# A state-space mixer and an expert network on one core: 68 identity transposes instead of 44 ahead of the last batch's row transposes

## What is computed

```
x = x + mixer(ctx_1024, layernorm(x))
x = x + ffn(layernorm(x))
```

```
scores = softmax(x @ gate_w.T);  topk_w, topk_i = top_k(scores, 6)
y = einsum('eci,eih->ech', silu(g) * u, w_down)
out = y summed over the 6 choices + silu(x @ sw_gate) * (x @ sw_up) @ sw_down
```

## Time and profile before

| | us |
|---|---|
| median of 3 executions | 1032.78 (1031.4 to 1037.14) |
| the profiled execution | 1031.32 |
| its span, first to last instruction | 1029.6 |
| TensorE matmul busy | 860.5 (84%) |
| VectorE busy | 603.9 (59%) |
| GpSimd busy | 565.4 (55%) |
| ScalarE busy | 498.0 (48%) |

### The profile page before, as it was taken

One profiled execution on the slowest core, in us unless ns is written; L12 is line 12 of the kernel. 1 busy time (PEld: TensorE's weight loads), 2 busy tenths in 40 slices (PEclk: granted clock), 3 DMA queues, 4 the chain that ended last, 5 costly groups with the idle time before them and its releaser, 6 DMA issues.

```text
span 1029.6 us, 12583 instructions
## 1 busy us (share of the span) xinstructions
PE 860.5 (84%) x4213; PEld 479.6 (47%) x4213; DVE 603.9 (59%) x862; ACT 498.0 (48%) x895; POOL 565.4 (55%) x318
## 2 busy tenths in 40 slices
PE   6375656667999786999789988999999988999984
PEld 3153445455455374545555474444444443444431
DVE  4589899889888988998798853222122211111111
ACT  4589545797776788766766223222122211221210
POOL 0387998987988988979777601122222212213111
PEclk9568655589899988999899979999999999999998
DMA  8633344334434553333637675999999999999995
GB/s 284 231 123 123 125 159 147 123 123 166 129 123 144 176 165 117 123 123 104 224 111 241 226 274 208 402 394 386 399 395 388 398 397 396 396 386 399 387 387 137
DMA packets 68411, 250.66 MB, mean 243 GB/s; under 512 B 10506, under 2 KB 13078, under 8 KB 68092
## 3 DMA queue, kind: packets, MB, share of 16 engines
q1 hardware_dynamic: 54740, 226.09, 58.4%
q0 software_dynamic: 7712, 18.88, 7.5%
q10 hardware_dynamic: 5896, 4.90, 1.5%
HBM read 230.67 MB, written 19.17 MB: 243 GB/s over the span
## 4 chain that ended last, share of the span: by engine, by line
PE 51%; DVE 16%; DMA 10%; issue 6%; ACT 6%; SPq 3%; POOL 2%; POOLq 0%; ACTq 0%; DVEq 0%
PE ps L683 13%; PE ps L886 10%; PE ps L678 9%; PE ps L694 8%; PE ps L910 6%; DVE ps L1272 6%; DMA arena<-in_L_ffn_w_down 5%; DVE arena L1279 4%; SPq L569 3%; DVE arena L1298 2%; ACT ps L1081 2%; PE ps L919 1%; DMA out_rows<-routes,idxs 1%; DVE arena L1272 1%; DMA out_rows<-xn,idxs 1%
## 5 line engine op out<-in xcount | busy, mean ns | idle before, releaser
L1516 POOL TENSOR_TENSOR arena<-arena 128x1024 f32<-128x1024 f32 x128 | 300.0, 2359 | 57.2 <-DMA arena<-bc_rows 40.0
L678 PE MATMUL ps<-ident,arena 128*128 128x128 f32 (+2 forms) x1408 | 238.5, 321 | 84.5 <-DVE ps L1280 39.8
L678 PEld LDWEIGHTS ps<-ident,arena 128*128 128x128 f32 (+2 forms) x1408 | 199.3, 177 | 190.1 <-issue 85.8
L1081 ACT ACTIVATE ps<-arena,An 128x511 f32<-128x511 f32 x256 | 165.2, 680 | 109.5 <-DVE ps L1280 93.4
L1272 DVE TENSOR_TENSOR_SCAN ps<-ps,arena 128x1024 f32<-128x1024 f32 x82 | 187.6, 2287 | 15.5 <-ACT ps L1081 14.7
L886 PE MATMUL ps<-arena 128*64 128x352 f32 x984 | 158.7, 461 | 7.7 <-issue 3.9
L683 PE MATMUL ps<-xnT,sw 128*128 128x512 f32 x320 | 152.1, 619 | 12.7 <-ACT arena L1042 11.8
L1530 POOL DMA_INDIRECT arena<-xn_rows,idu x32 | 34.1, 1066 | 208.6 <-DVE wcol L1426 149.1
L1521 POOL TENSOR_TENSOR arena<-arena 128x1024 f32<-128x1024 f32 x46 | 108.4, 2356 | 49.0 <-DVE arena L1272 49.0
L1433 DVE TENSOR_TENSOR arena<-arena,ps 128x352 f32<-128x352 f32 x32 | 16.7, 522 | 171.1 <-PE ps L886 171.1
L886 PEld LDWEIGHTS ps<-arena 128*64 128x64 f32 x984 | 73.2, 137 | 80.8 <-issue 71.3
(11 more groups left out here) (166 smaller groups left out, 903.6 us busy)
## 6 DMA issues: line engine op xcount, KB each, us to landing
arena<-bc_rows SPq DMA_DIRECT2D x128, 512.0 KB, 4.8
arena<-in_L_ffn_w_down SPq DMA_DIRECT2D x59, 768.0 KB, 23.0
arena<-in_L_ffn_w_gate SPq DMA_DIRECT2D x64, 704.0 KB, 23.5
arena<-in_L_ffn_w_up SPq DMA_DIRECT2D x59, 704.0 KB, 23.3
arena<-in_x SPq DMA_DIRECT2D x4, 1024.0 KB, 6.8
xn_rows<-xn ACTq DMA_DIRECT2D x4, 1024.0 KB, 6.4
out_rows<-arena SPq DMA_DIRECT2D x4, 1024.0 KB, 5.2
extra<-in_L_ffn_w_up SPq DMA_DIRECT2D x5, 704.0 KB, 22.3
```

Of the source, the lines that this page charges most:

```text
L678: return nc.tensor.matmul(dst, src, ident[0:k, 0:k], is_transpose=True, **kw)
L1081: a = nc.scalar.activation(ps[:, 2 * (c % 2) + n, 1:L], dt[k][:, 1:L], ACT.Exp, scale=An[:, k, NB * g + n:NB * g + n + 1])
L1516: G.tensor_tensor(R[c % RING], dtu[k][:, None, :].to_broadcast([P, NB, L]), Brep[n % REPS], ALU.mult)\
```

## The change

The constant that sets the number of transposes of the identity in the job `pe warm` goes from 44 to 68. Nothing else differs.

```
-TAILFILL = 44
+TAILFILL = 68
```

## The result

| | before | after |
|---|---|---|
| median, us (20 executions each) | 1032.42 (1027.42 to 1037.14) | 1027.56 (1025.07 to 1032.08) |
| ratio, 95% interval | | 0.9959 (0.9944 to 0.9975) |
| the profiled execution, us | 1031.32 | 1027.87 |
| its span, us | 1029.6 | 1026.1 |

The change makes the kernel faster, by 0.41%: 4.2 us by the ratio, 4.9 by the medians. I had forecast 1026.0 with a range of 1023.0 to 1033.5 and a gain of 6.0 us. The measured median is inside that range and just past the end of the forecast's own, narrower one (1023.5 to 1027.5).

A forecast was written before the change was run, and what follows sets the result against it. DMA bounds the expert stream, but its restart waits on TensorE's routing at half clock; profiled 1031.32 minus 6.0 gives 1025.3, with the median's offset 1026.8, forecast 1026.0 between; range 1023.0 to 1033.5, the forecast's own 1023.5 to 1027.5.

The forecast's parts named there:

- The mechanism: Before the last batch's row transposes: 24 added transposes fill TensorE's 2.45 us idle time, cost about 0, and prevent the clock's fall.
- the replay: Last batch's routing recalculated at full TensorE clock, from row transposes at 604.04 us to first tokens at 631.9, 6.0 us earlier.
- The score store: Last batch's store of scores, which the first gather awaits: starts right behind the row store, lands at 626.5 us.
- Rival (a): The score store still lands at 630.2 us and holds the first gather: tokens only 3.1 us earlier, time 1028.2; chance 0.18.
- So for about 13.6 us (...) a bound TensorE runs at 1.2 GHz instead of 2.4: Last batch's routing, 604.45 to 618.1 us: half clock while TensorE is the bound; removing it was to give 6.0 us.
- within 0.5%: Outcome class for the whole kernel's time: a change under some 5.2 us, not told from no change; chance 0.45.
- The idle time's length: TensorE's gaps before a clock fall: 2.22 us was followed by one, 1.93 us not; 2.45 us counted as falling side.
- Rival (c): The idle gap before the row transposes does not cause the low clock, so nothing is gained: 1031.3 us; chance 0.05.
- Rival (b): The clock falls anyway at 604 to 608 us, during row transposes and logits with short waits: 1031.3 us; chance 0.12.
- The expert stream passes an earlier start on: Expert weight stream: starting the first pair earlier ends the rest, same bytes at the same rate, earlier by the same amount.
- rival (d): Expert weight stream restarted at another moment meets other waits and loses half the gain: 1028.3 us; chance 0.05.
- slower rival (e): In the fill, TensorE is already at 1.2 GHz, so the 24 added transposes put 5.1 us on the path: 1036.4 us; chance 0.05.

## Why the prediction came out as it did

**The mechanism was right.** In the changed kernel's first profile the added transposes fill the idle time and cost nothing (7.59 us for 68, 7.6 forecast). The clock does not fall. From the row transposes to the mask's end it is 8.84 us (8.5 forecast), to the run of 20 9.19 (8.9), to the tokens 28.26 (27.9). The 0.3 us went in small waits for the copies before the logits' end; from there on the replay was right. Gain of the stage in this pair of profiles: 33.87 - 28.26 = 5.6 us, 6.0 forecast.

**The score store** was the sharpest test of the replay, and it came out 0.8 us late. I put its landing at 626.5 and it came at 626.6, but this profile starts the stage 0.63 us early, so that agreement is luck. Behind the first row transposes the landing was forecast at 22.5 us and came at 23.2, the gather at 23.4 and came at 24.3; its data took 3.9 us, not 3.5. The term that was too small is the time from the store's first packet to its landing, 7.2 us in the prediction: ScalarE's queue turns from the row store's large packets to the score store's small ones at about 618.5 (52 packets with 0.11 MB in 617 to 618, 47 with 0.04 MB in the next us, 71 with 0.02 MB in the one after), which leaves 8.1. The order that the Trainium skill's rule on rings gives (DMA: Bandwidth & Descriptors, Queues, rings and completion order), row store first, agrees with these packets; the rule gives no landing time. Standing behind the row store is not what makes this store slow: in the profile of before only 4 packets were left on the queue from 619.5 on, the store was issued at 619.73, and it still took 10.5 us. Rival (a) is wrong as priced (its own sum, 631.1 + 3.5, is 634.6 and not 634.8), but near: in two of the three profiles with 68 (1.04 and 0.83 us), and in those with 52 and 60, TensorE waits for the gather.

**The size was off, and the step is "So for about 13.6 us (...) a bound TensorE runs at 1.2 GHz instead of 2.4".** I read one profile and took its low stretch as the kernel's. Five profiles with 44 transposes show two cases: 13.6 us of low clock and 33.87 us to the tokens twice, 6.8 us and 30.8 to 31.3 three times. Against 28.4 us with 68, the mean of the three, that costs 5.5 us or 2.4 to 2.9. The mean of the five is 32.15, so the mean cost is 3.8 us; the means of all executions differ by 3.9 us (1031.4 - 1027.5, give or take 0.45), and the ratio of the change's own measurement is 4.2 us. The forecast of 6.0 us was the price of the worse case. By the prediction's own classes a gain of 0.41% belongs to "within 0.5%" (chance 0.45) and not to "faster" (0.50). That the kernel gains on the average execution what the five profiles average is shown as far as five profiles can; what decides which case an execution meets I could not find in the program.

**The idle time's length decides less than I said.** I had taken 1.93 us as harmless and 2.22 as harmful. In the first repeat of the kernel before, an idle time of 1.67 us in the expert phase was followed by a fall (first two fences, TensorE and the clock), and in the repeat with 68 one of 2.67 us was not (last two):

```profile
831.39 3.04 PE L910 MATMUL ps<-arena,routes 118*64 118x512 f32 x8 [1.67 <-DMA arena<-in_L_ffn_w_down]
```

```profile
832.50:835.50 3.00, 3.00 (x10) 0.86 (x6) 0.00 (x0) 0.00 (x0) 0.00 (x0) 0.50 1.02 407
```

```profile
1005.74 2.80 PE L910 MATMUL ps<-arena,routes 118*64 118x512 f32 x12 [2.67 <-DMA arena<-in_L_ffn_w_down]
```

```profile
1005.70:1010.00 4.30, 4.19 (x21) 1.82 (x21) 0.83 (x2) 0.53 (x1) 1.55 (x1) 1.00 0.28 103
```

Behind the 2.45 us ahead of the row transposes the fall came in five profiles of five, behind the 1.58 us with 52 transposes not in its one. Rival (c) is refuted by these rows: take the gap away or shorten it, and the fall in the routing is away, in all eight profiles with 52 or more transposes. The Trainium skill (TensorE: Matmul & The Clock Gate, HAM oscillation) warns about longer gaps only; these traces disagree. Rival (b) did not happen: logits and row transposes hold a full clock in all of those. Once the clock is low, the same work got it back after 6.8 us in three profiles with 44 and not for 13.6 us in two.

**The expert stream passes an earlier start on**, as I had said, within its own scatter. Over the fourteen profiles the time from SyncE's first refill to the end is 388.7 us in the mean, 386.9 to 390.2, and the end goes with the refill at a slope of 0.94, give or take 0.11. My profile of before happened to have one of the shortest streams (387.2) and that of after one of the longest (390.0); this is the 2.8 us that seemed lost, and rival (d) is not needed.

**The slower rival (e)** did not happen in any profile: the fill ran at 0.109 us a piece in each that has one.

**What stays open.** 140 transposes delay the tokens by 7.6 us against 68, and the times by 4.6 (means, give or take 0.5, partly from different chips) or 5.2 (ratios, whose intervals allow some 3 us either way), so whether such a delay reaches the end in full is not settled. A part may be that executions with 68 sometimes pay the 1.5 us of a fall behind a late gather, seen with 52 and 60. Two of my three profiles with 68 have the late gather, but none has the fall. The start of the fill itself lies between 594.6 and 599.0 us in the profiles, for reasons earlier in the kernel that I did not look into; 4.4 us of spread come from there alone. The spread of 10 us itself is only explained in part: the two cases of the low clock are 3 us apart, and the executions with 68, whose three profiles show no low clock in the routing, still spread from 1024.5 to 1032.1 us.

No tried number beats 68 clearly. 52 and 60 are as fast within their errors; 92 is 1.2 us slower, give or take 0.6, where the 24 transposes that it adds take 2.6.

## What to carry to other kernels

Before you price a low clock from one profile, look at it in several: where it falls and how long it stays differs from execution to execution, and the gain that counts is the mean over the cases. A fill that ends too early can be worth nothing, as the fall is only moved to where the engine is needed; make it reach close to the next real work, and stop there, since each further transpose is on the path. And when a stage gets shorter, work out when the DMA that ran beside it lands: here a 128 KB store beside the weight stream became the last to arrive in two of three profiles.

## What the runs showed of the hardware

- The same idle time of 2.45 us was followed by a low clock of 13.6 us twice and of 6.8 us three times. In the two long cases it fell 0.4 us behind the start of the row transposes, in the three short ones 0.2 us. During the long ones TensorE was busy without a pause (13.00 of 13.00 us) and the clock stayed low; in a short one it came back after 6.48 busy us of 6.50. Being busy alone does not tell when it returns.
- A low clock that begins in an idle time costs less: without a fill, 6.4 of the 13.6 us passed before the first row transposes (one profile).
- Idle times of 0.98 and 0.75 us, separated by 0.72 us of work, were followed by a fall (52 transposes; 1.10 and 0.75 us with 60 too), while 1.04 and 0.75 us at the same place (68 transposes) and a single one of 2.67 us elsewhere were not.
- A 128 KB store on ScalarE's queue, 2.0 us to landing in the median of the four batches, took 11.4 us in the last batch of the changed kernel, beside the weight stream and issued 9.8 us behind a 1 MB store of the same queue. Issued 13.7 us behind it (before) it took 10.5 us, and 17.6 us behind it (140 transposes) 6.2 us.
